# Linear attention's output beside the edge attention: the projection as three f32r products, context and divisor products joined, 18 K|V slots in place of 20

## The chip, the cores and the metric

The kernel runs on 1 core of one Trainium2 chip. The metric is the device time in microseconds of one execution; three runs of the kernel before took 3078.94, 3080.64 and 3082.0 us, median 3080.64.

## The reference

A graph layer of 3125 nodes with 512 features and 53125 edges: `x + gnn(layernorm(x)) + mix(layernorm(x))`, followed by a mixture of experts. `gnn` has two layers of edge attention. `mix` is a linear attention over all nodes, whose last part the change touches:

```python
q = softmax(proj(Wq, bq), axis=-1); k = softmax(proj(Wk, bk), axis=-1); v = proj(Wv, bv)
k_sum = k.sum(axis=2, keepdims=True)
D_inv = 1.0 / (q * k_sum).sum(axis=-1, keepdims=True)
context = jnp.einsum('bhtd,bhte->bhde', k, v)
out = jnp.einsum('bhtd,bhde->bhte', q, context) * D_inv + q
out = out.transpose(0, 2, 1, 3).reshape(B, T, H * D)
return out @ Wp.T + bp
```

In the graph layer each edge scores the query of its target against the key of its source; the scores are normalised over each target's edges and weigh the sources' values.

## The kernel before

**Stages.** Layer norm and the projections q, k, v of layer 0; the branch (projections of the linear attention, its context `BD`); the edge attention of layer 0; the join of split targets, the output projection and the feed-forward of layer 0; the same three for layer 1; the experts. Engines run their own programs and meet at semaphores.

**The edge attention** (`attend_*`, once for each layer). 53125 sorted edges lie in 416 chunks of 128 (`ET`), a group `g` is four chunks, so there are 104 groups (`NQ`). For each chunk POOL fetches 128 rows of K|V, 4 KB each, by an indirect DMA into a slot of a ring, `kvs` (`fetch`, L1096). The ring has `KVN = (20, 25)` slots in the two layers. `fetch(n)` with n >= KV waits on `agg` until the group that used the slot has been gathered, group (n - KV)//4. PE turns a chunk's keys (`turn_k`, L1179: four transposes), ACT and DVE empty them, PE makes masks and scores (L1197, L1209), DVE and ACT the softmax, PE turns the weights (L1186) and gathers the values from the ring's slots (`gather`, L1222: two parts of 16 products a group; the trace has 64 records for a group). In PE's loop over g the order of one turn is: turn two chunks, the second part of the gather of group g - 3 (its end counts up `agg`), turn two more chunks, slot table or queries, turn the weights, masks and scores, the first part of the gather of group g - 2. The chunks turned are 4g+2 to 4g+5 (`LOOK` is 2, `AGG_AT` is 2). POOL also fetches query rows (L1105) and scatters results (L1113), one of the two in each turn. In layer 0 the ring lies in `WA` (four slots), `G` (two), `Y` (twelve), `mt` and `rowsb`; six fetches go out early, ahead of the branch's end.

**The output of the linear attention** (`out_*`) goes beside the edge attention of layer 0, in pieces: each engine's program is a generator of 25 tiles x 16 steps, of which the edge loop takes four a turn (`next(side)`), so a tile takes four turns. For a tile of 128 nodes: SP loads q; step 0, PE turns q (L743) into PS[0], step 1 ACT copies it to `qT`; step 3, PE multiplies by the context, four f32 products of 128 columns (L762) and four of 2 columns for the divisor (L765); step 4, DVE takes the reciprocal (L791), multiplies (L793) and adds q (L796); step 7, PE turns the result; step 8, ACT copies it to `oT` (L819); steps 10 to 13, PE makes one f32 product of 512 columns each with `Wp` (L774); step 14, DVE adds the bias, and SP stores the tile. `Wp` is in `WA[:, 2]`, whose memory is also seen as `WA2r` in f32r; `WA[:, 1]` is also `WoH`.

**Cutting into high and low.** In other stages an f32 product is made as three f32r products: ACT copies an operand to f32r (high), DVE subtracts that from the operand (low), and PE adds high x high, high x low and low x high. The counts of the cut weights, `w_hi` and `w_lo`, run through the whole program, so later waits hold absolute numbers (`WO_CUT`, `qkv_pe`).

Of the kernel before, what the change touches and what calls it, by code (L numbers as in the profile page):

```python
# [6 lines left out]
P = 128  # L7
N, D, H, DH = 3125, 512, 8, 64
# [14 lines left out]
AGG_F = 3200  # L23
AGG_L = AGG_F + ET
AGG_ROWS = AGG_L + ET
KVN = (20, 25)
CAP = 16
MASK = 2.0 ** 100
LOOK = (2, 2)
# [5 lines left out]
F32 = mybir.dt.float32  # L35
# [4 lines left out]
ALU = mybir.AluOpType  # L40
ACT = mybir.ActivationFunctionType
# [27 lines left out]
def h8(ap):  # L69
    return ap.rearrange("p (h d) -> p h d", h=H)  # L70


def k4(ap):
    return ap.rearrange("p (k n) -> p k n", k=4)
# [6 lines left out]
def build(nc, A, out):  # L81
    with ExitStack() as ctx:
# [16 lines left out]
        mt = sb("mt", [P, 2584])  # L99
# [458 lines left out]
            return 2 * (u + 1) if u < NT else NT + u + 1  # L558

        def qkv_pe(l, xs, Wh, Wl, beside):  # L560
            pe.wait_ge(w_lo, (12, 40)[l])
            for u in range(2 * NT):
                r = ROWS[u % NT]
                pe.wait_ge(x_lo, TURN0[l] + u + 1)
                for w in ((1, 2) if u < NT else (0,)):
                    e = 2 * u + w - 1 if u < NT else NT + u
                    f = e - 4
                    if f >= 2 * NT:
                        pe.wait_ge(q_out, NT * l + f - 2 * NT + 1)
                    elif f >= 0:  # L570
                        pe.wait_ge(kv_out, 2 * NT * l + f + 1)
                    for k in range(4):
                        xh, xl = xs[:, u % 2, 0, k, 0:r], xs[:, u % 2, 1, k, 0:r]
                        pe.matmul(PS[e % 4][0:r, :], xh, Wh[:, w, k, :], start=(k == 0), stop=False)  # L574
                        pe.matmul(PS[e % 4][0:r, :], xh, Wl[:, w, k, :], start=False, stop=False)  # L575
                        mm = pe.matmul(PS[e % 4][0:r, :], xl, Wh[:, w, k, :], start=False, stop=(k == 3))  # L576
                    mm.then_inc(qkv_mm, 1)
                beside(u)
# [72 lines left out]
        def pair(G, i):  # L651
            return G[:, i:i + 2, :].rearrange("p a b -> p (a b)")

        def edge_views(Y, G, l):
            kvs = [Y[:, 1024 * i:1024 * (i + 1)] for i in range(12)]
            kT = [work[:, i, :] for i in range(3)]
            pT = [stage[:, 2, :]]
            spare = [WA[:, w, 2 * i:2 * i + 2, :].rearrange("p a b -> p (a b)") for w in range(3) for i in range(2)]
            if l == 0:
                kvs = spare[0:4] + [pair(G, i) for i in (0, 2)] + kvs + [mt[:, 512:1536], pair(rowsb, 2)]  # L660
                kT += [G[:, 12 + i, :] for i in range(3)]
            else:
                kvs = [mt[:, 512 + 1024 * i:1536 + 1024 * i] for i in range(2)] + [pair(rowsb, 2)] + spare + kvs + [
                    pair(G, i) for i in (0, 2, 10)] + [pair(rowsb, 0)]
                kT += [G[:, 12 + i, :] for i in range(4)]
            probs = [pair(G, i).rearrange("p (c h s) -> p c h s", c=4, h=H) for i in (4, 6)]
            qblk = [pair(G, 8).rearrange("p (k b s) -> p k b s", k=4, b=8), qblk1[:, :, :, :]]
            onehot = [Y[:, 12288 + P * i:12288 + P * (i + 1)] for i in range(2)]
            return kvs, probs, qblk, onehot, kT, pT
# [35 lines left out]
        m_b, b_read, m_st, mq_in = sem("m_b"), sem("b_read"), sem("m_st"), sem("mq_in")  # L705
        m_qf, m_qe, m_of, m_oe, m_c, m_out = sem("m_qf"), sem("m_qe"), sem("m_of"), sem("m_oe"), sem("m_c"), sem("m_out")
        OUT = 16

        def out_views(G):
            return k4(G[:, 10, :]), k4(G[:, 11, :]), G[:, 15, :], mt[:, 1536:2048], rowsb[:, 0, :], WA[:, 2]  # L710

        def fetch_q(t, qb):
            if t:
# [23 lines left out]
        def out_pe(views):  # L737
            qT, oT, qb, ob, outb, Wp = views

            def features(bank, t, buf, made):  # L740
                r = ROWS[t]
                for k in range(3):
                    pe.transpose(bank[:, k * P:k * P + r], buf[0:r, k * P:(k + 1) * P], ident[0:r, 0:r])  # L743
                pe.transpose(bank[:, 3 * P:3 * P + r], buf[0:r, 3 * P:4 * P], ident[0:r, 0:r]).then_inc(made, 1)

            yield
            pe.wait_ge(g_in, 16)
            pe.wait_ge(m_bd, 1)
            for s in range(OUT * NT):
                t, k = divmod(s, OUT)  # L750
                r = ROWS[t]
                if k == 0:
                    pe.wait_ge(mq_in, 16 * (t + 1))
                    if t:
                        pe.wait_ge(m_out, t)
                    features(PS[0], t, qb, m_qf)
                if k == 3:
                    pe.wait_ge(m_qe, t + 1)
                    if t:
                        pe.wait_ge(b_read, t)  # L760
                    for f in range(4):
                        pe.matmul(PS[0][0:r, P * f:P * (f + 1)], qT[:, f, 0:r], BD[:, f, 0:P], start=(f == 0),  # L762
                                  stop=(f == 3), skip_group_check=True)
                    for f in range(4):
                        mm = pe.matmul(PS[1][0:r, 2 * f:2 * f + 2], qT[:, f, 0:r], BD[:, f, P:P + 2], start=(f == 0),  # L765
                                       stop=(f == 3), skip_group_check=True)
                    mm.then_inc(m_c, 1)
                if k == 7:
                    pe.wait_ge(m_out, t + 1)
                    features(PS[1], t, ob, m_of)  # L770
                if k >= 10 and k < 14:
                    if k == 10:
                        pe.wait_ge(m_oe, t + 1)
                    mm = pe.matmul(PS[1][0:r, :], oT[:, k - 10, 0:r], Wp[:, k - 10, :], start=(k == 10), stop=(k == 13))  # L774
                    if k == 13:
                        mm.then_inc(m_b, 1)
                yield

        def out_dve(views):
            qT, oT, qb, ob, outb, Wp = views  # L780
            yield
            dve.wait_ge(row_in, 16 * 5)
            for s in range(OUT * NT):
                t, k = divmod(s, OUT)
                r = ROWS[t]
                di = small[0:r, 24:32]
                if k == 4:
                    dve.wait_ge(m_c, t + 1)
                    if t:
                        dve.wait_ge(m_of, t)  # L790
                    dve.reciprocal(di, PS[1][0:r, 0:8]).then_inc(*step_v.up())  # L791
                    dve.wait_ge(*step_v.now())
                    dve.tensor_tensor(h8(ob[0:r, :]), h8(PS[0][0:r, :]), di.unsqueeze(2).to_broadcast([r, H, DH]), ALU.mult  # L793
                                      ).then_inc(*step_v.up())
                    dve.wait_ge(*step_v.now())
                    dve.tensor_tensor(ob[0:r, :], ob[0:r, :], qb[0:r, :], ALU.add).then_inc(m_out, 1)  # L796
                if k == 14:
                    dve.wait_ge(m_b, t + 1)
                    if t:
                        dve.wait_ge(m_st, 16 * t)  # L800
                    dve.tensor_tensor(outb[0:r, :], PS[1][0:r, :], rowsb[0:r, 1, :], ALU.add).then_inc(b_read, 1)
                yield

        def out_act(views):
            qT, oT, qb, ob, outb, Wp = views
            yield
            for s in range(OUT * NT):
                t, k = divmod(s, OUT)
                r = ROWS[t]
                if k == 1:  # L810
                    act.wait_ge(m_qf, t + 1)
                    if t:
                        act.wait_ge(m_c, t)
                    act.activation(qT[:, :, 0:r], k4(PS[0][:, :])[:, :, 0:r], ACT.Copy).then_inc(m_qe, 1)
                if k == 8:
                    act.wait_ge(m_of, t + 1)
                    if t:
                        act.wait_ge(m_b, t)
                    act.activation(oT[:, :, 0:r], k4(PS[1][:, :])[:, :, 0:r], ACT.Copy).then_inc(m_oe, 1)  # L819
                yield  # L820

        def out_done(e):
# [261 lines left out]
        def attend_pool(l, begin):  # L1084
# [30 lines left out]
                                        in_=stage[:, 0, :], in_offset=None, bounds_check=AGG_ROWS - 1,  # L1115
                                        oob_is_err=False).then_inc(sct, 16)

            early = (6, 9)[l]
            for n in range(early):
                fetch(n)  # L1120
            tables_stored(pool, l)
# [690 lines left out]
        W1, W2 = WA[:, 2, 1, :].rearrange("p (k o) -> p k o", o=P), WA[:, 2, 0, :]  # L1812
        ag_lo = sem("ag_lo")
        WA_IN = [48 * (l + 2) for l in range(2)]
        WO_CUT = (24, 40)

        def wo_high(l):
            act.wait_ge(wa_in, WA_IN[l])
# [247 lines left out]

        def cut_dve(n):
            if n < 12:
                dve.wait_ge(w_hi, 28 + n + 1)
                dve.tensor_tensor(Wl1[:, n // 4, n % 4, :], Wraw[:, n // 4, n % 4, :],  # L2070
                                  Wh1[:, n // 4, n % 4, :].bitcast(F32), ALU.subtract).then_inc(w_lo, 1)

# [615 lines left out]
```

## Time and profile before

| | |
|---|---|
| median of three runs | 3080.64 us (3078.94 to 3082.0) |
| span of the profiled execution | 3095.6 us |
| PE busy | 2657.9 us, 86% |
| DVE, ACT, POOL busy | 1629.2, 1321.1, 1115.8 us |
| chain that ended last | PE 60%, DMA 16%, DVE 8%, POOL 7%, issue 6% |

The profiled execution is another one than the three timed runs; of it the profile gives the span from first to last instruction, 15.0 us above their median, and no time of its own beside that. The chain is followed back from the last instruction, at each step to what released it; "issue" is time for which the profile shows no wait. A PE that is busy isn't PE at its peak, since products overlap and their ends are modelled.

### The profile page before, as it was taken

How to read it: one execution, taken by the hardware profiler on the slowest of the kernel's cores; microseconds unless marked ns; L12 is line 12 of the kernel's file. 1: busy time of each engine (PE TensorE's matmuls, PEld its weight loads, DVE VectorE, ACT ScalarE, POOL GpSimd, SP SyncE). 2: the span in 40 equal slices, each digit the busy share in tenths (PEclk: the TensorE clock that was granted, in tenths of full speed). 3: DMA queues.
4: the chain of work that ended last, by engine and by line, in shares of the span. 5: the costliest groups of instructions: out<-in, count | busy, mean ns of one | idle time of the engine just before them, and what ended most of it. 6: DMA issues, size and time to landing. Idle time of an engine off the chain costs nothing.

```text
span 3095.6 us, 78344 instructions
## 1 busy us (share of the span) xinstructions
PE 2657.9 (86%) x32605; PEld 2143.5 (69%) x32605; DVE 1629.2 (53%) x3272; ACT 1321.1 (43%) x3690; POOL 1115.8 (36%) x1130
## 2 busy tenths in 40 slices
PE   5999997999999999758899788888888678599998
PEld 4877885777777777546488577777777465477777
DVE  5236785555555555456512355555554645656553
ACT  3324443555555555422232255555555322333432
POOL 0000002666666666400001267777777111222110
PEclk8999998999999999979999899999999889799998
DMA  5642003988899998641024489999999431122211
GB/s 195 228 175 107 31 28 140 317 313 316 309 331 322 317 325 297 222 121 41 14 97 154 160 321 354 352 349 347 350 347 352 126 113 57 38 89 92 69 59 58
DMA packets 231795, 621.75 MB, mean 201 GB/s; under 512 B 39008, under 2 KB 45792, under 8 KB 231427
## 3 DMA queue, kind: packets, MB, share of 16 engines
q0 software_dynamic: 137088, 466.78, 42.2%
q1 hardware_dynamic: 94339, 149.78, 14.6%
q8 instruction: 265, 4.34, 0.6%
q14 instruction: 103, 0.84, 0.1%
HBM read 538.80 MB, written 103.39 MB: 207 GB/s over the span
## 4 chain that ended last, share of the span: by engine, by line
PE 60%; DMA 16%; DVE 8%; POOL 7%; issue 6%; ACT 2%; SPq 0%; DVEq 0%; POOLq 0%; ACTq 0%
PE ps L1179 6%; DMA Y<-KVd,srcE 5%; PE ps L574 5%; PE ps L575 4%; PE ps L576 4%; DMA aggd<-stage,segs 4%; PE ps L1222 4%; PE ps L1209 4%; PE ps L774 3%; POOL Y L1096 3%; PE ps L942 2%; PE ps L944 2%; PE ps L943 2%; PE ps L1186 2%; PE ps L1872 2%
## 5 line engine op out<-in xcount | busy, mean ns | idle before, releaser
L1096 POOL DMA_INDIRECT Y<-KVd,srcE x449 | 430.2, 958 | 230.6 <-issue 115.8
L1370 ACT ACTIVATE stage<-ps,stage 128x128 f32<-128x128 f32 x832 | 294.8, 366 | 115.3 <-PE ps L1186 112.4
L1096 POOL DMA_INDIRECT WA<-KVd,srcE x186 | 179.3, 964 | 361.8 <-PE ps L576 268.1
L1351 ACT ACTIVATE work<-ps 128x512 f32<-128x512 f32 x309 | 179.8, 597 | 303.8 <-PE ps L1179 303.5
L1179 PE MATMUL ps<-ident,Y 128*128 128x128 f32 x1796 | 252.2, 280 | 32.2 <-DMA Y<-KVd,srcE 26.8
L1351 ACT ACTIVATE G<-ps 128x512 f32<-128x512 f32 x315 | 181.8, 597 | 223.5 <-PE ps L1179 223.1
L1277 DVE COPY G<-ps 128x512 f32<-128x512 f32 x208 | 143.8, 691 | 245.8 <-PE ps L1186 243.0
L574 PE MATMUL ps<-Wh,xs 128*128 128x512 f32 x600 | 238.7, 398 | 31.2 <-DVE xs L514 31.2
L1179 PEld LDWEIGHTS ps<-ident,Y 128*128 128x128 f32 x1796 | 199.2, 143 | 70.5 <-issue 49.3
L575 PE MATMUL ps<-Wl,xs 128*128 128x512 f32 x600 | 236.9, 395 | 0.0
L576 PE MATMUL ps<-Wh,xs 128*128 128x512 f32 x600 | 236.5, 394 | 0.0
L1282 DVE TENSOR_REDUCE stage<-ps 128x4 f32<-128x512 f32 x208 | 143.9, 692 | 144.7 <-PE ps L1209 144.7
L1105 POOL DMA_INDIRECT stage<-Qd,segs x104 | 107.2, 1031 | 302.5 <-DVE segs L893 195.3
L1222 PE MATMUL ps<-Y,G 128*32 128x64 f32 x7184 | 188.5, 222 | 5.3 <-issue 2.8
L514 DVE TENSOR_TENSOR xs<-xT,xs 128x512 fp32r<-128x512 f32 (+1 forms) x100 | 67.8, 679 | 235.3 <-ACT xs L539 235.3
L1222 PEld LDWEIGHTS ps<-Y,G 128*32 128x32 f32 x7184 | 156.1, 111 | 25.6 <-issue 22.3
L1096 POOL DMA_INDIRECT mt<-KVd,srcE x54 | 51.4, 953 | 336.3 <-DMA Qd<-stage 319.2
L1370 ACT ACTIVATION_READ_ACCUMULATOR stage<-ps,stage 128x1 f32 x832 | 169.1, 203 | 0.0
L574 PEld LDWEIGHTS ps<-Wh,xs 128*128 128x128 f32 x600 | 113.0, 188 | 57.7 <-issue 24.2
L1296 DVE TENSOR_TENSOR stage<-stage,st 128x512 f32<-128x512 f32 x208 | 144.0, 692 | 7.1
L1186 PE MATMUL ps<-ident,stage 128*128 128x128 f32 x832 | 134.1, 286 | 3.4 <-DVE stage L1296 2.9
L1302 DVE COPY stage<-ps 128x512 f32<-128x512 f32 x104 | 71.9, 691 | 119.9 <-DMA aggd<-stage,segs 77.1
(383 smaller groups left out, 6775.2 us busy)
## 6 DMA issues: line engine op xcount, KB each, us to landing
KVd<-stage SPq DMA_DIRECT2D x96, 256.0 KB, 2.0
aggd<-work SPq DMA_DIRECT2D x6, 2048.0 KB, 7.4
Qd<-stage SPq DMA_DIRECT2D x48, 256.0 KB, 2.0
G<-aggd SPq DMA_DIRECT2D x48, 256.0 KB, 2.7
Y<-KVd,srcE POOLq DMA_INDIRECT x449
Y<-in_x SPq DMA_DIRECT2D x4, 1536.0 KB, 14.7
G<-mixq SPq DMA_DIRECT2D x24, 256.0 KB
mixd<-rowsb SPq DMA_DIRECT2D x24, 256.0 KB
```

The lines of the kernel that those rows point to most:

```text
L574: pe.matmul(PS[e % 4][0:r, :], xh, Wh[:, w, k, :], start=(k == 0), stop=False)
L575: pe.matmul(PS[e % 4][0:r, :], xh, Wl[:, w, k, :], start=False, stop=False)
L576: mm = pe.matmul(PS[e % 4][0:r, :], xl, Wh[:, w, k, :], start=False, stop=(k == 3))
L1096: pool.indirect_dma_start(out=kvs[a], out_offset=None, in_=KVd[l][:, :], in_offset=bass.IndirectOffsetOnAxis(ap=srcE[:, n:n + 1], axis=0)) ...
L1179: mm = pe.transpose(bank[:, k * P:(k + 1) * P], kvs[a][:, k * P:(k + 1) * P], ident[:, :])
L1186: mm = pe.transpose(bank[:, i * P:(i + 1) * P], pT[g % len(pT)][:, i * P:(i + 1) * P], ident[:, :])
L1222: mm = pe.matmul(AG[32 * i:32 * i + 32, DH * h:DH * (h + 1)], probs[x][:, i, h, :], kvs[a][:, D + DH * h:D + DH * (h + 1)], start=(x == 0 ...
L1277: dve.tensor_copy(probs[x][:, :, :, CAP * x:CAP * (x + 1)], bank[:, :].rearrange("p (c h s) -> p c h s", c=4, h=H)).then_inc(out_d, 1)
L1282: dve.tensor_reduce(smin[:, 4 * g:4 * g + 4], SC[g % 2][:, :].rearrange("p (c e) -> p c e", c=4), AXX, ALU.min).then_inc(mins, 1)
L1296: dve.tensor_tensor(p4, p4, rec4[:, :].unsqueeze(2).to_broadcast([P, 4, P]), ALU.mult).then_inc(normed, 1)
L1351: act.activation(kT[n % len(kT)], banks(l)[place_of(l, "k", n) % len(banks(l))][:, :], ACT.Copy).then_inc(out_a, 1)
L1370: last = act.activation(pT[g % len(pT)][:, P * i:P * (i + 1)], SC[g % 2][:, P * i:P * (i + 1)], ACT.Exp, bias=smin[:, t:t + 1], scale=-1.0 ...
```

## The change

The projection's weights are cut once, in the first tile: `WpH` takes the memory of `WA[:, 1]`, `WpL` is written in place over `Wp`. The tile's result is cut too, high by ACT and low by DVE, into two parts of `G` that held `qT` and `oT`; `qT` moves to `fx3`. Each of the four projection steps then makes three f32r products. The context and divisor products are joined to 130 columns, three in PS[0] and one in PS[1]; DVE's reciprocal and multiplication are each split accordingly. Since `WA[:, 1]` is taken, the ring of layer 0 loses two slots: 18, and four early fetches. The counts of cut weights that come later move by 4.

```diff
-KVN = (20, 25)
+KVN = (18, 25)
...
-            pe.wait_ge(w_lo, (12, 40)[l])
+            pe.wait_ge(w_lo, (12, 44)[l])
...
-                kvs = spare[0:4] + [pair(G, i) for i in (0, 2)] + kvs + [mt[:, 512:1536], pair(rowsb, 2)]
+                kvs = spare[0:2] + [pair(G, i) for i in (0, 2)] + kvs + [mt[:, 512:1536], pair(rowsb, 2)]
...
+        WpH, WpL, WP_CUT = WoH, WA2r, 24
 
         def out_views(G):
-            return k4(G[:, 10, :]), k4(G[:, 11, :]), G[:, 15, :], mt[:, 1536:2048], rowsb[:, 0, :], WA[:, 2]
+            return k4(fx3[:, :]), (k4(partH[:, 2, :]), k4(partH[:, 3, :])), G[:, 15, :], mt[:, 1536:2048], rowsb[:, 0, :], WA[:, 2]
...
-                    for f in range(4):
-                        pe.matmul(PS[0][0:r, P * f:P * (f + 1)], qT[:, f, 0:r], BD[:, f, 0:P], start=(f == 0),
-                                  stop=(f == 3), skip_group_check=True)
-                    for f in range(4):
-                        mm = pe.matmul(PS[1][0:r, 2 * f:2 * f + 2], qT[:, f, 0:r], BD[:, f, P:P + 2], start=(f == 0),
-                                       stop=(f == 3), skip_group_check=True)
-                    mm.then_inc(m_c, 1)
+                    for f in range(3):
+                        pe.matmul(PS[0][0:r, 130 * f:130 * (f + 1)], qT[:, f, 0:r], BD[:, f, :], start=(f == 0),
+                                  stop=(f == 2), skip_group_check=True)
+                    pe.matmul(PS[1][0:r, 0:130], qT[:, 3, 0:r], BD[:, 3, :], start=True, stop=True,
+                              skip_group_check=True).then_inc(m_c, 1)
...
-                    if k == 10:
-                        pe.wait_ge(m_oe, t + 1)
-                    mm = pe.matmul(PS[1][0:r, :], oT[:, k - 10, 0:r], Wp[:, k - 10, :], start=(k == 10), stop=(k == 13))
+                    i = k - 10
+                    if i == 0:
+                        pe.wait_ge(m_oe, 2 * t + 2)
+                    if t == 0:
+                        pe.wait_ge(w_lo, WP_CUT + i + 1)
+                    hi, lo = oT[0][:, i, 0:r], oT[1][:, i, 0:r]
+                    pe.matmul(PS[1][0:r, :], hi, WpH[:, i, :], start=(i == 0), stop=False)
+                    pe.matmul(PS[1][0:r, :], hi, WpL[:, i, :], start=False, stop=False)
+                    mm = pe.matmul(PS[1][0:r, :], lo, WpH[:, i, :], start=False, stop=(i == 3))
...
-                    dve.reciprocal(di, PS[1][0:r, 0:8]).then_inc(*step_v.up())
+                    wide = PS[0][0:r, 0:390].rearrange("p (f n) -> p f n", f=3)
+                    dve.reciprocal(di[:, 0:6].rearrange("p (f x) -> p f x", f=3), wide[:, :, P:P + 2]).then_inc(*step_v.up())
+                    dve.reciprocal(di[:, 6:8], PS[1][0:r, P:P + 2]).then_inc(*step_v.up())
                     dve.wait_ge(*step_v.now())
-                    dve.tensor_tensor(h8(ob[0:r, :]), h8(PS[0][0:r, :]), di.unsqueeze(2).to_broadcast([r, H, DH]), ALU.mult
-                                      ).then_inc(*step_v.up())
+                    o4 = ob[0:r, :].rearrange("p (f x d) -> p f x d", f=4, x=2)
+                    dve.tensor_tensor(o4[:, 0:3], wide[:, :, 0:P].rearrange("p f (x d) -> p f x d", x=2),
+                                      di[:, 0:6].rearrange("p (f x) -> p f x", f=3).unsqueeze(3).to_broadcast([r, 3, 2, DH]),
+                                      ALU.mult).then_inc(*step_v.up())
+                    dve.tensor_tensor(o4[:, 3], PS[1][0:r, 0:P].rearrange("p (x d) -> p x d", x=2),
+                                      di[:, 6:8].unsqueeze(2).to_broadcast([r, 2, DH]), ALU.mult).then_inc(*step_v.up())
...
+                if t == 0 and k in (3, 5, 6, 7):
+                    i = (3, 5, 6, 7).index(k)
+                    dve.wait_ge(w_hi, WP_CUT + i + 1)
+                    dve.tensor_tensor(WpL[:, i, :], Wp[:, i, :], WpH[:, i, :].bitcast(F32), ALU.subtract).then_inc(w_lo, 1)
+                if k == 9:
+                    dve.wait_ge(m_oe, 2 * t + 1)
+                    dve.tensor_tensor(oT[1][:, :, 0:r], k4(PS[1][:, :])[:, :, 0:r], oT[0][:, :, 0:r].bitcast(F32), ALU.subtract
+                                      ).then_inc(m_oe, 1)
...
-                    act.activation(oT[:, :, 0:r], k4(PS[1][:, :])[:, :, 0:r], ACT.Copy).then_inc(m_oe, 1)
+                    act.activation(oT[0][:, :, 0:r], k4(PS[1][:, :])[:, :, 0:r], ACT.Copy).then_inc(m_oe, 1)
+                if t == 0 and 2 <= k < 6:
+                    if k == 2:
+                        act.wait_ge(g_in, 16)
+                    act.activation(WpH[:, k - 2, :], Wp[:, k - 2, :], ACT.Copy).then_inc(w_hi, 1)
...
-            early = (6, 9)[l]
+            early = (4, 9)[l]
...
-        WO_CUT = (24, 40)
+        WO_CUT = (28, 44)
```

## Rows read from the trace of the kernel before

**Rows 1.** The page: its first line, and the chain's shares by engine.

```profile
span 3095.6 us, 78344 instructions
...
PE 60%; DMA 16%; DVE 8%; POOL 7%; issue 6%; ACT 2%; SPq 0%; DVEq 0%; POOLq 0%; ACTq 0%
```

**Rows 2.** Stretches: length, busy us of PE PEld DVE ACT POOL, clock, DMA, GB/s.

```profile
498.00:520.00 22.00, 5.41 (x31) 4.88 (x29) 2.99 (x13) 2.27 (x4) 14.31 (x15) 0.50 0.90 329
560.00:900.00 340.00, 313.47 (x5899) 256.03 (x5888) 183.69 (x407) 179.47 (x561) 217.74 (x226) 0.98 0.90 316
...
1790.00:2090.00 300.00, 255.29 (x5766) 222.74 (x5765) 159.13 (x308) 175.27 (x565) 228.56 (x234) 0.97 0.96 348
```

**Rows 3.** Stretches, the gather's line L1222 alone: PE and PEld busy (records).

```profile
560.00:900.00 340.00, 58.32 (x2873) 48.06 (x2861) 0.98 0.90 316
900.00:1240.00 340.00, 60.48 (x2912) 49.38 (x2912) 0.99 0.90 316
```

**Rows 4.** The chain in order of time, 600 to 640: start us, us, what.

```profile
615.24 0.26 issue
615.50 0.96 POOL WA L1096
616.46 0.31 issue
616.76 5.52 DMA WA<-KVd,srcE
622.28 0.14 issue
622.41 0.63 PE ps L1179 x4
...
628.22 0.87 PE ps L1179 x8
629.09 0.63 PE ps L1222 x32
```

**Rows 5.** The chain's K|V fetches, four of the 34 from 540 to 1270.

```profile
946.47 6.00 DMA Y<-KVd,srcE
...
992.16 6.40 DMA WA<-KVd,srcE
...
1184.86 5.14 DMA G<-KVd,srcE
...
1213.81 8.89 DMA WA<-KVd,srcE
```

**Rows 6.** Timeline of PE: start us, us, line, operation, tiles, shapes, records.

```profile
400.37 0.39 PE L942 MATMUL ps<-Mh,xs 128*128 128x512 f32 x1
...
401.05 0.39 PE L942 MATMUL ps<-Mh,xs 128*128 128x512 f32 x1
...
597.44 1.98 PE L774 MATMUL ps<-WA,G 128*128 128x512 f32 x4
599.26 0.93 PE L1179 MATMUL ps<-ident,Y 128*128 128x128 f32 x7
...
702.78 0.95 PE L765 MATMUL ps<-mt,G 128*128 128x2 f32 x8
703.59 1.07 PE L1179 MATMUL ps<-ident,WA 128*128 128x128 f32 x8
```

**Rows 7.** Groups by line: shapes, count | busy us, mean ns | idle before, releaser.

```profile
L1967 DVE TENSOR_TENSOR aggL<-ps,aggH 128x512 fp32r<-128x512 f32 (+1 forms) x26 | 17.0, 655 | 32.5 <-ACT aggH L1906 32.5
...
L819 ACT ACTIVATE G<-ps 128x512 f32<-128x512 f32 (+1 forms) x25 | 14.7, 590 | 1.0 <-PE ps L744 1.0
...
L791 DVE RECIPROCAL small<-ps 128x8 f32<-128x8 f32 (+1 forms) x25 | 5.2, 207 | 20.1 <-PE ps L765 20.1
```

**Rows 8.** The chain where the edge stage begins.

```profile
499.06 7.69 DMA mixq<-rowsb
...
506.77 11.42 DMA G<-mixq
```

More of the change, by code:

```diff
@@ L2068, in cut_dve @@
             if n < 12:
-                dve.wait_ge(w_hi, 28 + n + 1)
+                dve.wait_ge(w_hi, WO_CUT[0] + 4 + n + 1)
                 dve.tensor_tensor(Wl1[:, n // 4, n % 4, :], Wraw[:, n // 4, n % 4, :],
```

## The prediction

> **What bounds the kernel now.** I read the page first, then the stretches, then the chain of waits inside the stretch that the diff touches. The page's chain runs 60% over PE and 16% over DMA [rows 1]. These are averages over stages, and the diff touches one stage: the edge attention of layer 0, from about 500 to 1300 us, beside which the linear attention's output runs. There PE is busy 313.47 of 340 us, and the DMA engines 0.90; in layer 1, which has the same edge work and no output beside it, PE is busy 255.29 of 300 us and the DMA engines 0.96 [rows 2]. The gather at L1222 leaves 64 records in each group of four chunks, so the counts give the length of one turn of the loop: 2873/64 = 44.9 and 2912/64 = 45.5 turns in 340 us each, 7.52 us a turn on the mean [rows 3].
>
> What ends last in a turn is to be seen in the chain [rows 4]. A gather ends at 615.25 and so gives back ring slots; POOL issues the first fetch after it (0.26, 0.96), then the second (0.31); that one lands 5.52 us after its issue; 0.14 us later PE turns it (622.41); PE's own work runs on to the next gather on the chain, which ends at 629.72. So about half of this two-turn loop is PE's work, and half is one fetch in flight. The chain between 540 and 1270 us passes through 34 such fetches: the middle one takes 6.00 us, the shortest 5.14 and the longest 8.89 [rows 4, 5]. PE is nearly full and the ring is already waited for: a shorter PE buys time only as far as the ring gives chunks sooner, and a shorter ring takes time directly.
>
> **The change part by part.** *Projection.* Before, one f32 product of 512 columns leaves two records; four records go from 597.44 to 599.26, so one product takes 0.91 us [rows 6]. After, it is three f32r products. Those of the branch start at 400.37 and, three later, at 401.05: 0.68 us for three, each with its own weight load in it [rows 6]. That is 0.23 us less in each of 4 products, 0.92 us a tile.
>
> *Context and divisor.* The four two-column products end with the next line's start: 702.78 to 703.59, 0.81 us a tile [rows 6]. They go away; the four wide ones gain 2 columns in 128, under 0.03 us together. So PE loses 1.7 us in each of 25 tiles, 43 us in all, 0.43 us in each turn (a tile takes four turns). This is the most that the change can give.
>
> *DVE and ACT.* DVE gains one reciprocal (0.21), one division split in two (between nothing and a whole second pass, which is as long as a subtraction) and one subtraction for the low half (0.66 for the like in a later stage), so 0.9 to 1.5 us a tile [rows 7]. DVE is busy 183.69 of 340 us [rows 2], so this lies beside idle time of 3.4 us a turn. The subtraction adds a wait: DVE waits for ACT's copy (0.59 [rows 7]), and behind it in DVE's queue stand the copies and minima of the running group, for which PE's next matmuls wait. ACT gets that copy at the head of a turn and DVE reaches the subtraction only after emptying a chunk that PE turns later, so I take nothing; without that cover the whole of it is 1.5 us x 25 = 38 us. PE's own wait for it comes after four more turned chunks, 0.87 us for each two [rows 4], so I take nothing there too.
>
> *Cutting the weights*, once: four ACT copies and four DVE subtractions, 4 x 0.59 + 4 x 0.66 = 5.0 us at most [rows 7]. They start with the first tile, while the ring is still full of first fetches; I take 0 and keep 5 for the range. The two early fetches that go move behind the branch: two issues of 1.27 us [rows 4], while the chain stands in the store and load of the first query tile, 7.69 and 11.42 us [rows 8]. No cost. The counts moved in the waits (w_hi, w_lo) keep their order. SP's queue gets nothing new.
>
> *The ring, 20 to 18 slots.* This decides. The gather of group q ends in turn q+3, just after the second of that turn's four chunks is turned. With 20 slots the four chunks that it lets POOL fetch, 4q+20 to 4q+23, are due as third and fourth chunk of the next turn and first and second of the turn after it. With 18 slots they are 4q+18 to 4q+21, due as first to fourth of the next turn. So the second fetch, which is now turned just behind the next gather [rows 4], must in the changed kernel be there just ahead of it. The loop closes in one turn, whatever PE has to do else: gather's end, 0.26 + 0.96 + 0.31 to the second issue, the fetch, 0.14, then the second chunk and the gather. The last two are half of 0.87 and 0.63 [rows 4], 1.1 us. The turn can't be shorter than 2.77 us + fetch. With the middle fetch of 6.0 that is 8.77 us; with 5.52 [rows 4] it is 8.29, with 6.40 [rows 5] it is 9.17. The third and fourth fetch are issued 1.27 and 2.54 us later and due after the gather; with the same 6.0 they make the fourth chunk late too, but inside the same 8.8 us. All of PE's work of a turn, 313.47/44.9 = 7.0 us now and 6.6 after, then lies beside the fetch: PE's 43 us go into waits.
>
> How long a fetch takes with fewer in flight isn't shown directly. A bound from below is the shortest, 5.14; from above the longest, 8.89 [rows 5]. I take 6.0, since the chain shows these second fetches at it and POOL will still issue four in a row; the pieces are picked by the chain, so if anything they lean to the slow.
>
> *Sum.* 398 of 416 chunks wait for a slot, so 100 turns get longer by 8.77 - 7.52 = 1.25 us: +125 us; PE's 43 us give nothing besides. The profiled span is 3095.6 us [rows 1], which gives 3220.6; it lies 15.0 us above the runs' median, so against 3080.64 the forecast is 3205.6 us.
>
> The Trainium skill prices a POOL-issued transfer otherwise: "DMA: Bandwidth & Descriptors", section "Anatomy of one DMA", has 2.0 us + bytes/436e3, an estimate of 3.2 us for the 512 KB of one fetch. By it the turn's bound would be 2.77 + 3.2 = 6.0 us, below PE's 6.6, and the smaller ring would cost nothing. The 34 fetches on the chain, none under 5.14 us [rows 5], speak against it here.
>
> **The rivals.** *The ring hides* (faster). Were a fetch to land in under 6.6 - 2.77 = 3.8 us once fewer are in flight, the loop through the ring would be shorter than PE's work and the change would give PE's saving: 3080.6 - 43 = 3038 us. For it: the DMA engines are busy 0.90, and a queue would drain. Against it: the shortest piece is 5.14 [rows 5]. Chance 0.08. The Trainium skill's fit, named above, would make this the outcome.
>
> *The fetch gets somewhat shorter*: 4.75 to 5.4 us gives turns of 7.52 to 8.17, 0 to +65 us, 3080 to 3145. For it: the drained engines. Chance 0.12, of which 0.04 lies within 0.2%.
>
> *PE's clock falls.* PE would be busy 6.6 of 8.77 us, 75%, with waits at several chunks. The granted clock is 0.98 in the edge stage of layer 0, 0.97 in layer 1 at a busy share of 85%, and 0.50 (the level of 1.2 GHz) from 498 to 520 us, where PE was busy 5.41 of 22 us [rows 2]. At the lower level all the time the 1.1 us on the loop would double: +110 us more, 3316. Between shares I don't expect it. Chance 0.05, 3255 to 3320.
>
> *The products aren't quicker than said* changes nothing in the forecast, since PE's work is hidden; it would take away only the gain of the first rival.
>
> **How the numbers follow.** Forecast 3205.6, chance 0.75, its own range from fetches of 5.52 (+77 us) and 6.40 (+165, and the 5 us of the cut weights): 3158 to 3250. For 8 in 10 I reach into the second rival: 3115 to 3250 leaves out the first rival (0.08), about half of the second (0.06) and the clock (0.05), 0.19 together. A measurement of this kernel can tell about 0.2% from no change, 6 us. Faster: 0.08. Same: 0.04. Slower: the rest, 0.88.
>
> **What would show it.** In 340 us inside the edge stage of layer 0 the gather's line should leave some 64 x 340/8.77 = 2480 records where it leaves 2873 now; the chain should pass through one fetch in each turn, with its piece near 6 us, and hold fewer of PE's projection; PE should wait most for the second and fourth chunk of a turn; traffic should fall from 316 GB/s [rows 2] to about 271. The f32 projection's 0.91 us should be 0.68, the two-column products gone. Layer 1 should stand as before. I am wrong if the turn stays under 7.6 us, if the chain there has no fetches, or if fetches land in 4 us.

## The result and the profile after

The changed kernel takes 3242.9 us (median of four runs, 3229.76 to 3252.79) against 3081.32 us of the kernel before on the same chip (3078.94 to 3082.43): ratio 1.0517 [1.0495, 1.0539], slower by 161.6 us. The forecast was 3205.6 us, slower by 125. Its profiled run is the quickest of the four, with a span of 3228.4 us; that is 132.8 us more than the profiled span of before [rows 1].

The page after, its span and its chain of waits; shares are of the span:

```profile
span 3228.4 us, 78228 instructions
...
PE 52%; DMA 22%; POOL 9%; issue 7%; DVE 7%; ACT 2%; SPq 1%; POOLq 0%; DVEq 0%; ACTq 0%
```

Against the chain of before (PE 60%, DMA 16% [rows 1]), DMA has six points more of a longer span, and PE eight fewer. The stretches show where (busy us of PE, PEld, DVE, ACT and POOL, then the granted clock, the DMA share and GB/s):

```profile
560.00:900.00 340.00, 268.38 (x4955) 225.10 (x4954) 161.38 (x368) 154.14 (x475) 180.74 (x189) 0.94 0.79 265
900.00:1240.00 340.00, 266.46 (x5045) 223.21 (x5045) 165.06 (x377) 159.22 (x488) 184.57 (x194) 0.96 0.81 272
...
1930.00:2230.00 300.00, 253.78 (x5789) 222.04 (x5790) 158.65 (x305) 174.93 (x565) 228.39 (x235) 0.97 0.97 350
```

Before, the first of these held 313.47 us of PE, a DMA share of 0.90 and 316 GB/s [rows 2]. Now PE is busy 45 us less of the same 340 us, and the DMA engines are idle a fifth of the time: each waits for the other. The third row is layer 1's edge stage, which the diff leaves alone; it reads as it did before [rows 2], only later in the run.

The gather's line alone (L1245 after, L1222 before), PE and PEld busy, with its records in brackets:

```profile
560.00:900.00 340.00, 50.16 (x2432) 41.93 (x2432) 0.94 0.79 265
900.00:1240.00 340.00, 51.06 (x2464) 42.69 (x2464) 0.96 0.81 272
```

Sixty-four records a turn: (2432 + 2464)/64 = 76.5 turns in 680 us, 8.89 us a turn, where it was 7.52 [rows 3]. Over the hundred turns of the stage that is +137 us, which is the growth of the span to 4 us. The first gather ends at 539.5 us where it ended at 540.3, so nothing was lost ahead of the loop: the whole loss lies in it.

What ends last in a turn is in the chain of waits. Two turns of it, in order of time (start, length, what; L763 and L765 are the joined products, L1202 turns a chunk's keys, L777 to L779 are the three f32r products of a projection step, L1245 is the gather, L1119 the fetch):

```profile
629.37 0.87 PE ps L763 x6
630.24 0.23 PE ps L765 x2
...
631.46 0.63 PE ps L1245 x32
632.08 0.26 issue
632.34 0.95 POOL Y L1119
633.30 0.31 issue
633.60 0.94 POOL Y L1119
634.54 0.30 issue
634.84 0.94 POOL Y L1119
635.78 0.30 issue
636.09 6.75 DMA Y<-KVd,srcE
642.84 0.14 issue
642.98 0.63 PE ps L1202 x4
...
644.60 0.23 PE ps L777
644.83 0.23 PE ps L778
645.06 0.23 PE ps L779
...
649.50 0.63 PE ps L1245 x32
...
654.15 7.08 DMA Y<-KVd,srcE
```

A gather ends at 632.09. POOL then issues three fetches, and the chain leaves it over the *fourth* (4.00 us after the gather), not over the second as in the loop of [rows 4]. That fetch takes 6.75 us, PE waits for it (0.14), and then 7.15 us of PE's work runs, to the end of the next gather on the chain at 650.13. 4.00 + 6.75 + 0.14 + 7.15 = 18.04 us for two turns, 9.02 us each. The next fetch on the chain takes 7.08. The chain passes through 64 fetches of K|V between 540 and 1440 us, where there were 34 before [rows 5]. Not all of them are fourth ones: counted by their place in the row, 27 are second fetches, 11 third and 26 fourth; before, nearly all were second ones. The shortest and the longest:

```profile
1226.23 5.25 DMA G<-KVd,srcE
...
1342.79 8.00 DMA WA<-KVd,srcE
```

PE's waits for fetches, in 560 to 1240 us (line, what it waited for: us in total, times, longest):

```profile
PE ps L1202 <- DMA Y<-KVd,srcE: 80.2, 76, 3.2
PE ps L1202 <- DMA G<-KVd,srcE: 21.0, 17, 2.4
PE ps L1202 <- DMA WA<-KVd,srcE: 13.3, 12, 1.8
```

In the kernel before, the same three lines of the same stretch were:

```profile
PE ps L1179 <- DMA Y<-KVd,srcE: 20.3, 25, 2.9
PE ps L1179 <- DMA WA<-KVd,srcE: 8.4, 7, 2.3
PE ps L1179 <- DMA G<-KVd,srcE: 6.1, 7, 2.1
```

There the waits under these three slot names came to 35 us, now to 115.

By place in the row, over the whole stage, from the semaphore records of the two traces (fetches that wait for a slot, some 100 of each place; us from the start of the issue to the landing, medians; and PE's idle time ahead of a chunk whose data had not landed, in us, with the number of times):

| | first | second | third | fourth |
|---|---|---|---|---|
| fetch, before | 5.43 | 6.05 | 6.52 | 6.78 |
| fetch, after | 4.42 | 5.47 | 6.14 | 6.51 |
| PE idle, before | 8 (9) | 38 (42) | 0 (0) | 0 (1) |
| PE idle, after | 7 (9) | 68 (56) | 32 (46) | 81 (82) |

For the first fetch many landing records are incomplete; the complete ones alone give 5.72 before and 4.53 after.

### The profile page after: what moved, and what is told of

It reads as the page before. It is cut to its first block, busy times and chain, and to the rows that moved or that the text cites. A ratio compares the mean times of both kernels' runs of the same rounds, so it can differ in the third digit from the quotient of the medians.

```text
span 3228.4 us, 78228 instructions
## 1 busy us (share of the span) xinstructions
PE 2665.5 (83%) x32505; PEld 2162.6 (67%) x32505; DVE 1646.2 (51%) x3351; ACT 1327.5 (41%) x3694; POOL 1106.8 (34%) x1130
## 4 chain that ended last, share of the span: by engine, by line
PE 52%; DMA 22%; POOL 9%; issue 7%; DVE 7%; ACT 2%; SPq 1%; POOLq 0%; DVEq 0%; ACTq 0%
DMA Y<-KVd,srcE 9%; PE ps L1202 5%; POOL Y L1119 4%; PE ps L574 4%; PE ps L576 4%; PE ps L575 4%; DMA aggd<-stage,segs 4%; PE ps L1245 3%; PE ps L1232 3%; PE ps L965 2%; PE ps L967 2%; PE ps L966 2%; POOL WA L1119 2%; DMA G<-KVd,srcE 2%; DMA stage<-Qd,segs 2%
## 5 line engine op out<-in xcount | busy, mean ns | idle before, releaser
L1119 POOL DMA_INDIRECT Y<-KVd,srcE x475 | 451.4, 950 | 344.6 <-PE ps L1245 196.5
L1202 PE MATMUL ps<-ident,Y 128*128 128x128 f32 x1900 | 282.9, 285 | 124.3 <-DMA Y<-KVd,srcE 104.6
L1202 PEld LDWEIGHTS ps<-ident,Y 128*128 128x128 f32 x1900 | 213.3, 144 | 169.4 <-issue 98.0
L1119 POOL DMA_INDIRECT WA<-KVd,srcE x150 | 145.1, 967 | 355.6 <-PE ps L576 266.5
L1245 PE MATMUL ps<-Y,G 128*32 128x64 f32 x7600 | 187.7, 224 | 6.1 <-issue 4.4
L1119 POOL DMA_INDIRECT mt<-KVd,srcE x57 | 54.3, 952 | 361.5 <-DMA Qd<-stage 320.2
L1245 PEld LDWEIGHTS ps<-Y,G 128*32 128x32 f32 x7600 | 156.5, 112 | 27.8 <-issue 24.9
```

The lines of the kernel that those rows point to most:

```text
L1119: pool.indirect_dma_start(out=kvs[a], out_offset=None, in_=KVd[l][:, :], in_offset=bass.IndirectOffsetOnAxis(ap=srcE[:, n:n + 1], axis=0)) ...
L1202: mm = pe.transpose(bank[:, k * P:(k + 1) * P], kvs[a][:, k * P:(k + 1) * P], ident[:, :])
L1245: mm = pe.matmul(AG[32 * i:32 * i + 32, DH * h:DH * (h + 1)], probs[x][:, i, h, :], kvs[a][:, D + DH * h:D + DH * (h + 1)], start=(x == 0 ...
```

## The experiments

Line numbers are each kernel's own: the gather is L1222 in ring18, ring19 and ring21, L1251 in new20, L1245 in gfirst18, L1247 in the kernels with a filler and L1226 in join21g. Ratios are to the kernel before, on the same chip.

### The two halves apart: ring18 and new20

*ring18* is the kernel before with the smaller ring and nothing else:

```diff
-KVN = (20, 25)
+KVN = (18, 25)
...
-                kvs = spare[0:4] + ...
+                kvs = spare[0:2] + ...
...
-            early = (6, 9)[l]
+            early = (4, 9)[l]
```

> The kernel before with 18 slots in layer 0's ring and four early fetches, and nothing else of the change. Theory R (the ring's loop sets the turn: gather's end, two issues, fetch, second chunk, gather): the old products' longer PE work still fits beside the fetch, so the time is that of the changed kernel, 3215 to 3260 us. Theory W (the change's own work, DVE's added subtraction and waits or three products with a weight load each, made the turn longer): slots cost nothing, 3081 us within 10.

Measured: 3278.54 us, ratio 1.0643 [1.0617, 1.0669], +197.5 us: some 19 us above the range of theory R, and far from theory W. Its gather (same columns as above):

```profile
560.00:900.00 340.00, 49.38 (x2368) 41.38 (x2368) 0.93 0.78 260
900.00:1240.00 340.00, 47.18 (x2304) 39.35 (x2304) 0.90 0.76 252
```

73 turns in 680 us, 9.32 us each. The ring alone costs more than the whole change.

*new20* is the change with 20 slots kept; the operands that stood in the two slots go to parts of `partH`, `rowsb` and `fx3` that are idle then. Some of them now share a buffer by turns, so DVE and ACT have a few waits more than in the change (not shown here):

```diff
-KVN = (18, 25)
+KVN = (20, 25)
...
-                kvs = spare[0:2] + [pair(G, i) for i in (0, 2)] + kvs + [mt[:, 512:1536], pair(rowsb, 2)]
+                kvs = spare[0:4] + [pair(G, i) for i in (0, 2)] + kvs + [mt[:, 0:1024], mt[:, 1024:2048]]
...
-        WpH, WpL, WP_CUT = WoH, WA2r, 24
+        WpH, WpL, WP_CUT = [partH[:, 2, :], partH[:, 3, :], rowsbR[:, 2, :], rowsbR[:, 3, :]], WA2r, 24
...
-            early = (4, 9)[l]
+            early = (6, 9)[l]
```

> The changed kernel with 20 slots: the cut weights' high half goes to two parts of G and two of rowsb, the tile's rows share fx3 and rowsb's first row by turns, which frees room for two slots. All products and DVE work as in the changed kernel. Theory R: as the kernel before or up to PE's saving faster, 3038 to 3081 us; about half of its turns are bound by the ring, so near 3060. Theory W: 3243 us within 15.

Measured: 3062.25 us, ratio 0.9928 [0.9903, 0.9953], -19 us, as theory R said. The gather leaves 3008 records in each of the two stretches, 7.23 us a turn, at a clock of 0.99:

```profile
560.00:900.00 340.00, 61.12 (x3008) 50.45 (x3008) 0.99 0.92 330
```

So the ring is the cause of the loss and the products are a gain. But the two don't add up: +197 and -19 make 178, and the change costs 162. With 18 slots the products are worth 3278.5 - 3242.9 = 36 us, with 20 slots 19. Both kernels with the short ring ran at a lower clock, which comes up below.

### The length of the ring: ring19 and ring21

*ring19* and *ring21* are the kernel before with other lengths: 19 slots with five early fetches, and 21 slots, where the division's result `ob` leaves `mt` for `fx3` and `mt` gives a slot more:

```diff
-KVN = (20, 25)
+KVN = (21, 25)
...
-... + kvs + [mt[:, 512:1536], pair(rowsb, 2)]
+... + kvs + [mt[:, 0:1024], mt[:, 1024:2048], pair(rowsb, 2)]
...
-            return ..., G[:, 15, :], mt[:, 1536:2048], rowsb[:, 0, :], WA[:, 2]
+            return ..., G[:, 15, :], fx3[:, :], rowsb[:, 0, :], WA[:, 2]
```

> The kernel before with 19 slots (one slot of WA less, five early fetches), no other change. Theory R2 (what closes the loop is the last fetch that is due in the next turn, over two turns: its issue and landing, then PE's work from that chunk to the gather of the turn after): with 19 slots that is the third fetch, 2.8 + 6.15 + 0.14, then 0.5 + 4.2 + 1.6 of PE, 15.4 us for two turns, 7.7 a turn against 7.3 with 20 slots and 8.7 with 18 at the full clock: 3105 to 3140 us. If each slot costs the same (half of what 18 cost): 3180 us. If the ring is only too short from 18 on: 3081 us.

Measured: 3180.03 us, ratio 1.0295 [1.0261, 1.0328], +99.6 us: a miss for R2, which had 3105 to 3140, and what the rule "each slot costs the same" had said. The gather of ring19:

```profile
560.00:900.00 340.00, 52.33 (x2528) 43.78 (x2528) 0.94 0.80 279
900.00:1240.00 340.00, 51.65 (x2528) 42.72 (x2528) 0.93 0.80 279
```

39.5 turns in 340 us, 8.61 us each, at a clock of 0.94 and 0.93. One slot costs half of what two cost. R2 took 6.3 us for PE's work from the awaited chunk to the end of the next gather; the chain of before shows 7.31 us there (622.41 to 629.72 [rows 4]). With that, and 6.39 us for the third fetch (its median in ring19), the same sum gives 8.3 us a turn, an estimate; so a part of the miss was PE's share of the loop.

> The kernel before with 21 slots (the tile's rows go to fx3, and mt holds two slots), no other change. Theory R: the second fetch is now due as the first chunk of the turn after the next, 4 us later, and the first one behind the next gather; the ring binds no turn, which then takes PE's 7.0 us: 3081 - 100 x 0.4 to 0.5, 3030 to 3045 us. If 20 slots were enough: 3081 us within 10.

Measured: 3059.94 us, ratio 0.9925 [0.9903, 0.9946], by the ratio some -23 us: a gain, though short of the forecast. Its gather's clock is 1.00 throughout:

```profile
560.00:900.00 340.00, 61.09 (x2976) 50.23 (x2976) 1.00 0.94 328
900.00:1240.00 340.00, 61.41 (x3032) 50.85 (x3036) 1.00 0.93 330
```

7.24 us a turn on the mean, where I had counted on PE's 7.0. From 18 to 21 slots the ratios are 1.064, 1.030, 1 and 0.993: the nineteenth and the twentieth slot are worth some 100 us each, the twenty-first 23.

### The gather earlier, and the clock: gfirst18, filler18, gf18fill, fill23

If the loop is what the chain shows, it gets shorter when the gather, which frees the slots, comes earlier in the turn. *gfirst18* is the change with the gather of a turn ahead of that turn's chunks, in layer 0 alone:

```diff
+                if l == 0 and g > AGG_AT:
+                    gather(g - 1 - AGG_AT, 1)
...
-                        if g > AGG_AT:
+                        if l and g > AGG_AT:
```

*filler18* leaves the order and asks for the clock instead: ahead of each wait for a fetch PE makes one f32 product of 256 columns, a filler, into the bank that the turned chunk will overwrite. It is extra work; nothing of the result uses it:

```diff
+                if l == 0:
+                    pe.matmul(bank[:, 0:256], ident[:, :], xT[:, 0, 0:256], start=True, stop=True, skip_group_check=True)
```

*gf18fill* has both. *fill23* is filler18 with the product only ahead of two of a turn's four chunks, the third and the fourth (`if l == 0 and n % 4 in (0, 1)`).

> The changed kernel, 18 slots, with one thing moved in PE's order of layer 0: the second part of the gather comes ahead of the turn's first two chunks and not behind them. Slots come back about 1 us earlier in the turn, and the second fetch is due behind the next gather. Theory R: the loop over the second fetch falls to 1.56 + 5.5 + 0.14 - 0.5 = 6.7 us, the one over the fourth, 4.05 + 6.5 + 0.14 + 0.5 + 4 over two turns, to 7.6 a turn; so some 7.6 us a turn where the changed kernel has 8.9: about 3110 us, 3060 to 3140. Theory W: 3243 us within 15, as no work is taken away.

Measured: 3249.27 us, ratio 1.0525 [1.0486, 1.0564]: no gain, a clear miss.

> The changed kernel with one product of 256 columns added ahead of PE's wait for each chunk of layer 0, written into the bank that the chunk is turned into next, four in a turn, about 0.43 us each; it stands where PE waits for the fetch. Theory C (a part of the slowdown, some 35 us, comes from PE's clock falling to the lower level in the waits): the granted clock in the stage rises from 0.95 to 0.98 and the time falls to about 3210 us. Theory R alone: the added work hides in the waits or nearly, clock or not, 3243 to 3270 us. If PE's work of a turn set the time, 4 x 0.43 x 104 = 180 us more, 3420 us.

Measured: 3248.74 us, ratio 1.0538 [1.051, 1.0565]: no gain either, though the clock came back (below).

> The changed kernel with the second part of the gather ahead of the turn's chunks and a filler product of 256 columns ahead of each of the four waits for a chunk, to hold PE's clock in the waits. Without the filler the turns came in pairs, 12.4 and 5.9 us, with the clock granted at 0.87 to 0.89 and 215 us of the stage at the lower level. Theory R with C (the moved gather does shorten the loop through the ring, and the fall of the clock in the long waits ate that): clock 0.97 or more, turns of 7.6 to 8.1 us, 3110 to 3160 us. Theory W, or a loop through the ring that doesn't go over the gather's place: 3245 us or above, as filler alone left it.

Measured: 3171.24 us, ratio 1.029 [1.026, 1.0319]: a gain with the clock back, though 11 us above the range of R with C.

> The changed kernel with the filler product only ahead of the turn's third and fourth chunk, where PE waits for the third and fourth fetch. There it lies in the wait, off the loop over the fourth fetch; ahead of all four chunks it added 0.4 us to a turn (two fillers on that loop in two turns) and gave the clock back, which cancelled. Theory C: the clock comes back (0.97) without that price, and the turn goes from 8.9 to 8.6 us: 3205 to 3220 us. If the clock costs nothing: 3243 us within 12 or above.

Measured: 3213.94 us, ratio 1.0419 [1.0397, 1.0442], as theory C said; the profiled run is the longest of its five, at 3231.19.

The first four together, as ratios:

| | as it was | with the filler |
|---|---|---|
| gather where it was | 1.0517 (the change) | 1.0538 (filler18) |
| gather first | 1.0525 (gfirst18) | 1.029 (gf18fill) |

Neither edit gives anything alone; both together give back 70 us. The stretch from 560 to 900 us says why. All engines, first gfirst18, then gf18fill:

```profile
560.00:900.00 340.00, 282.16 (x4829) 236.57 (x4828) 159.02 (x359) 151.54 (x465) 179.15 (x189) 0.87 0.74 263
```

```profile
560.00:900.00 340.00, 330.81 (x5594) 283.64 (x5592) 173.72 (x396) 165.16 (x505) 194.07 (x203) 0.99 0.85 284
```

The gather alone, of gfirst18, filler18, gf18fill and fill23, in this order:

```profile
560.00:900.00 340.00, 51.14 (x2368) 43.12 (x2368) 0.87 0.74 263
```

```profile
560.00:900.00 340.00, 47.97 (x2368) 39.94 (x2368) 0.98 0.79 261
```

```profile
560.00:900.00 340.00, 52.54 (x2592) 43.37 (x2592) 0.99 0.85 284
```

```profile
560.00:900.00 340.00, 50.91 (x2496) 42.31 (x2496) 0.98 0.82 272
```

gfirst18 makes as few turns as filler18, 37 in 340 us, but at a clock of 0.87: what the shorter loop saved, the clock took. The chain of gfirst18 shows one slow turn beside a normal one:

```profile
645.51 1.01 PE ps L1232 x32
...
679.32 0.43 PE ps L779
...
680.19 1.87 PE ps L1232 x32
```

The same 32 products of L1232 take 1.01 us in the one and 1.87 in the other, and one projection product (L779) takes 0.43, against 0.23 at full clock. With the filler the clock is 0.98 to 0.99, and the turns differ by order alone: 340/37 = 9.19 us in filler18, 340/40.5 = 8.40 in gf18fill. There PE is busy 330.81 of 340 us, so PE with its fillers is nearly the bound. filler18 got nothing for its better clock, and the likely reason is that its products stand on the loop too. Its chain, up to a gather that frees slots:

```profile
631.50 0.43 PE ps L1201 x2
631.93 0.44 PE ps L1204 x4
632.37 0.43 PE ps L1201 x2
632.80 0.44 PE ps L1204 x4
633.24 0.63 PE ps L1247 x32
```

The two products (L1201) ahead of the first and second chunk take 0.86 us between the data and the gather that frees the next slots. fill23 takes those two away, keeps 0.98 of clock and is 29 us quicker than the change by the medians (1.0419 against 1.0517). So some 29 us of the change's loss go back to its clock. That the fillers act through the clock alone is argued, since all that they add is PE's work; if the two that remain cost time, the clock's share is larger.

### The products apart and a kernel that uses what was found: joined20, f32r20, new20g, join21g

*joined20* is the kernel before with the joined context and divisor products alone; *f32r20* is new20 with the old, separate ones, so the f32r projection alone, with the places and waits of new20. Their products are the two parts of the diff above.

> The kernel before, 20 slots, with the context and divisor products joined to 130 columns and nothing else. PE loses 0.8 us a tile, 20 us in all; half of the turns are bound by the ring. Expected 3081 less 5 to 15 us. If PE's work doesn't count at 20 slots: 3081 us within 4; if DVE's split division eats it: above 3081.

Measured: 3080.53 us, ratio 0.999 [0.9971, 1.0008]: nothing that can be told from the noise, where a little was expected.

> The changed kernel with 20 slots and the old context and divisor products: the projection as three f32r products alone. PE loses 0.92 us a tile, 23 us in all. Expected 3081 less 5 to 15 us; with joined20 together about the 19 us that both gave at 20 slots. If the cut of the rows by DVE (0.66 us a tile and its wait) eats it: 3081 us or above.

Measured: 3075.52 us, ratio 0.9968 [0.995, 0.9987]. That is the upper end of what was expected. Together (new20) they give 0.7%, apart 0.1% and 0.3%; the intervals leave open whether together is more than the sum.

*new20g* is new20 with gfirst18's order; *join21g* is ring21 with the joined products and that order, and with the projection left in f32.

> The changed kernel's products with 20 slots, and the second part of the gather ahead of the turn's chunks. Theory R: with both, the second fetch is due a chunk and more behind its landing (X + 7.7 against a turn + 1.5), so the ring binds no turn and PE's work sets it: 6.6 to 6.9 us a turn, 3005 to 3040 us. If what is left in the 20-slot version isn't the ring: 3062 us within 10.

Measured: 3053.87 us, ratio 0.9907 [0.9882, 0.9933]: a miss. It is 8 us below new20 by the medians, with intervals that overlap, and so within the 10 us of the other outcome named, that what is left with 20 slots isn't the ring. PE was busy 316.46 of 340 us there, in turns of 7.1 us and not 6.6 to 6.9.

> The kernel before with 21 slots, the joined context and divisor products and the second part of the gather ahead of the turn's chunks; the projection stays f32. The ring binds no turn, so PE's work counts: against 21 slots alone (3060 us) less 10 to 20 us for the joined products: 3040 to 3050 us, ahead of the f32r version with 20 slots and the same order (3054 us). If something else than ring and PE sets those turns: 3060 us within 6.

Measured: 3047.51 us, ratio 0.9872 [0.9847, 0.9898], inside what was expected, and quicker than both kernels. Its gather:

```profile
560.00:900.00 340.00, 64.43 (x3072) 52.56 (x3072) 0.99 0.94 338
```

48 turns in 340 us, 7.08 us each, at 338 GB/s. From new20g it can't be told apart (the intervals overlap): with 21 slots the f32 projection does no worse than the f32r one with 20.

## Why the prediction was right, and where it was not

**The bound and the direction held.** The forecast said that the ring decides and the products don't, and ring18 (+197 us) and new20 (-19) show it by undoing one part at a time. The numbers asked for beforehand: about 2480 records of the gather (2432 and 2464), a turn of 8.77 us (8.89), traffic of about 271 GB/s (265 and 272), layer 1 as before (253.78 of 300 us, clock 0.97). The products are as quick as said: three f32r products take 0.23 us each in the change's chain (L777 to L779 above) against 0.91 for one f32 [rows 6], and context with divisor takes 0.87 + 0.23 = 1.10 us (L763, L765 above) where the chain of before has

```profile
611.81 1.09 PE ps L762 x8
612.89 0.79 PE ps L765 x8
```

Of the signs named, one failed: the chain was to pass through one fetch in each turn, and it passes through 64 in some 100 turns, since a loop over the fourth fetch takes two. PE waits most for the second and fourth chunk, as said.

**"The third and fourth fetch ... inside the same 8.8 us" failed.** It rested on one length, 6.0 us, for all four fetches of a row. By the table above the second, third and fourth took 5.47, 6.14 and 6.51 us in the changed kernel. So the loop that I had priced, over the second fetch, would close in 2.77 + 5.47 = 8.2 us. The loop that I had put inside it, over the fourth, takes 18.04 us for two turns on the chain, 9.0 us a turn; PE stood idle for 82 of 99 fourth chunks, 81 us, and for 56 of 100 second ones, 68 us. The measured turn, 8.89 us, lies between the two, and that it stands so close to 8.77 is in part chance.

The two-turn loop isn't new. The loop of [rows 4] is the same one: it runs through the chunk that a turn takes fourth, which with 20 slots is the second fetch of a row, and with 18 the fourth. Worked out from the pieces of one loop each, with the median fetch, it gives (1.52 + 6.05 + 0.14 + 7.31)/2 = 7.5 us a turn before and (4.00 + 6.51 + 0.14 + 7.15)/2 = 8.9 after, an estimate; 7.52 and 8.89 were measured. So the smaller ring costs two issues more on POOL, 2.48 us, and 0.46 us more of fetch, in every two turns.

**"PE's 43 us go into waits" failed with it.** On the loop over the second fetch PE has 1.1 us, on that over the fourth it has a whole turn's work, 7.15 of 18.04 us. Of the products' 0.43 us a turn half is then on the path where that loop binds, 21 us in a hundred turns; ring18 against the change shows 36 us. The rest of it isn't settled; ring18's lower clock (0.93 and 0.90, against 0.94 and 0.96) would account for some.

**The ring's term was too small**, 125 us against 197 with the old products. Since the products gave 36 where I put nothing, two errors of opposite sign left a forecast 37 us short by the medians: that it came as near as that is luck. Seen by the profiled runs alone it is 8 us short: the span grew by 132.8 us. The other 29 are the choice of runs, since the profiled span of before lay 15 us above the median of its runs and that of after 14.5 us below its own; a term worked out from one execution is no better than that.

**The clock was treated as all or nothing.** I gave it 0.05, for a fall of the whole stage to the lower level. It fell in pieces: 0.94 and 0.96 on the mean where it was 0.98 [rows 2]. One piece (stretches of the changed kernel, columns as above):

```profile
590.00:604.00 14.00, 7.82 (x168) 6.42 (x168) 5.90 (x11) 5.07 (x15) 6.88 (x9) 1.00 0.81 266
604.00:611.00 7.00, 6.33 (x65) 5.19 (x67) 1.45 (x5) 2.70 (x10) 2.68 (x3) 0.53 0.81 292
611.00:618.00 7.00, 7.00 (x117) 5.93 (x113) 2.71 (x5) 2.54 (x5) 2.41 (x3) 0.98 0.16 42
```

PE was busy 7.82 of 14 us at a granted clock of 1.00, then worked through 7 us at 0.53 (the level of 1.2 GHz), then had 0.98 again. The chain passes through those 7 us. By fill23 it costs some 29 us of the 162, and gfirst18, at 0.87 with its turns in long and short pairs, shows that it can cost more. ring19 ran at 0.94 and 0.93; that the clock makes up what PE's share leaves of its miss is argued from those rows and wasn't tried with a filler.

**The first rival** (a fetch under 3.8 us) fell: no fetch on the chain is under 5.25 us, and the shortest of all that wait for a slot, a first one of its row, took 4.18 by its complete record. The fit that speaks for it, in the Trainium skill ("DMA: Bandwidth & Descriptors", section "Anatomy of one DMA — SWDGE (gpsimd) path"), gives 3.2 us for one fetch, an estimate; no stretch of a run here shows one by itself. With two slots fewer in flight the pieces on the chain still ran from 5.25 to 8.00. **The second** (4.75 to 5.4 us) was nearly right about the second fetch, 5.47 us, and wrong about the time, since the loop over the fourth is longer.

**DVE, ACT, the cutting of the weights**: new20 has all of them and is quicker than the kernel before, so with 20 slots they cost less than the products give; that they cost nothing isn't shown. The new subtraction takes 0.68 us on the median of its 25, a little over the 0.66 that I had taken for it.

**What stays open.** Whether a long turn falls to the lower level because it was long, or becomes long because the level fell, is told apart only by the fillers, and only for the mean. Fillers smaller than 256 columns, or behind ring19, weren't tried. The quicker f32r projection beside 21 slots wasn't built, for it needs room that the slots take.

## What to carry to other kernels

Before trading buffer slots for a quicker product, walk every fetch of the row around the loop, the last one as well, with its own measured length: a slot less puts the chunk that closes the loop later in the row, behind more issues and with a longer fetch, and here two slots of 20 cost 197 us where the products could give 43 at most. Waits of TensorE that look free can also lower its clock, here from 0.98 to 0.94, so give the sum a term for it, and price it by the rows of a stretch with like waits. And when an edit gives nothing, look whether two effects have cancelled: moving the gather showed its worth only when the clock was held up.

## What the runs showed of the hardware

- Of four indirect fetches of 128 rows of 4 KB, issued in a row, each takes longer on the median than the one ahead of it, and the last ones hardly shorten when the DMA engines are less busy: as their share fell from 0.90 to 0.79, the medians from issue to landing went from 5.43 to 4.42 us for the first of a row, 6.05 to 5.47 for the second, 6.52 to 6.14 for the third and 6.78 to 6.51 for the fourth.
- The granted clock of TensorE fell to 0.53 for some 7 us after a stretch in which it was busy 7.82 of 14 us, inside a stage whose mean stayed at 0.94, and single f32 products of 256 columns in the waits brought the mean back to 0.98 (filler18 and fill23).
- A lower clock can hide the gain of an edit in full: gfirst18 made 2368 records of the gather in the stretch at 0.87, gf18fill, with more work on PE, 2592 at 0.99.
